# The second four images of an attention-weighted 3x3 convolution computed with four products per pair of output columns, on factor images made by GpSimd

## Chip, cores and metric

The kernel runs on one core of a Trainium2 chip. The metric is the device time of one execution in microseconds (us). A core has the engines TensorE (PE; its weight loads are listed as PEld), VectorE (DVE), ScalarE (ACT), GpSimd (POOL) and SyncE (SP), which here issues nearly all DMAs. All data are float32.

## What is computed

`x` has the shape (8, 32, 64, 64): 8 images, 32 channels, 64x64 pixels. Two stages follow each other, both with a residual. The first is a spectral convolution on the lowest 32x32 modes; the change doesn't touch it. The second is a 3x3 convolution whose kernel is mixed for every image from 16 kernels by an attention over the image's mean:

```
x = x + spectral_conv(group_norm(x))
v = group_norm(x)                                   # one group per channel
att = softmax(sigmoid(mean_hw(v) @ ksm_w.T))        # (8, 16)
kernels = clip(ifft2(sum_k att[b,k] * dft_weight[k]).real, -10, 10)
x = x + (conv3x3(v, kernels, padding=1) + bias) * fbm_scale
```

## The kernel before

**Layout.** After the spectral stage the result lies as `xa` (in `y_buf`): partition 32j + c holds channel c of the image rows 4u + j (u from 0 to 15), 66 columns per row with a padding column at each end. `xb` (in `w_buf`) is `xa` with the partition halves swapped and shifted by one row group, made by two DMAs per image; with both, a product reaches three image rows in four matrix products that run side by side, each on 32 rows of output partitions. The images are worked in two groups of four, g = 0 (images 0 to 3) and g = 1 (images 4 to 7): statistics, attention, aggregated kernel, weights, and then the convolution, one image after the other.

**The convolution** (`conv(b, n)`, line 1043) forms output columns in pairs with five products. Product n = 0 is shared by both columns: the middle kernel column on `sa` = pixel 1 + pixel 2 of each pair (made by GpSimd, in `x_buf`; its swapped copy lies in `t_buf` or `r_buf`). n = 1 is two more terms for the even columns, n = 2 two more for the odd ones, read from `xa` and `xb` at every second column. A term is eight matrix instructions of 512 columns (four row blocks, two passes for float32). The results go in turn into six PSUM banks (`conv_bank`). ScalarE takes product 0 with the bias into `shared` (`out_copy`, line 556); VectorE adds it to products 1 and 2 and writes the output rows in `bd_buf` (`out_copy`, line 816, two per image).

**What sets the order.** Each engine has its own list of work, written by hand, and the lists meet in semaphores. On TensorE: the inverse transforms i1 and i2 of the first stage, the small products of group 0's attention, its aggregation (line 1001), then `conv` of the images 0 to 7. Between the products of the images 0 to 3 stand group 1's small products: `sum_rows(1)` (line 982), `logits(1)` (line 987, waits for `pool_ready`, which VectorE's line 728 gives), `spread(1)` (line 993, waits for `num_ready`, given by line 752), `aggregate(1)` (line 1001), `mean_through_kernels(1)` (line 1009). TensorE waits at each of these in its order. On VectorE, the steps of a group's attention are `variance` (lines 716 to 719), `pooled` (724 to 728), `scales` (732 to 740), `sigmoid` (745, 746), `by_group` (752), `attention` (760), then `kernels` (770 to 780) and the weight copies (794). Most of them are tiny, and each waits for the one before. Between `variance(1)` and `pooled(1)` stands `out_copy(0)`.

GpSimd, after the work on the 16 kernels, forms `sa` in four instructions of two images each (line 441). SP issues in this order: loads; for the images 0, 2, 1, 3 the copies to `xb`; their `sa` copies; copies to `xb` and of `sa` for 4, 6 and then 5, 7; then all stores, four of 128 KB per image (line 307), each image once VectorE has counted `out_dve` up to it. The last image is stored in halves, two of its four stores per half from ScalarE's queue.

## Time and profile before

| | |
|---|---|
| median of 3 runs | 139.88 us (139.41 to 140.42) |
| the profiled execution | 140.62 us |
| span in its profile, first to last instruction | 138.8 us |
| granted TensorE clock, mean | 0.995 |
| TensorE busy | 122.7 us (88%) |
| VectorE busy | 88.0 us (63%) |
| ScalarE busy | 70.7 us (51%) |
| GpSimd busy | 52.6 us (38%) |
| convolution, first to last product | about 94.2 to 134.7 us |

All times within the run are us from the start of the span. Busy time of an engine counts its instructions' spans, without the time in which it waits for a semaphore. An instruction that has been issued and is held up by a resource shows as a longer instruction.

### The profile page before, as it was taken

Reading aid. Unit: us, or ns where it says so; the run is one execution under the profiler, and the core shown is the slowest. Engines: PE = TensorE matmul, PEld = TensorE weight load, DVE = VectorE, ACT = ScalarE, POOL = GpSimd, SP = SyncE. Lnnn points to the kernel's source line nnn. Section 1 sums busy time; section 2 is a strip of 40 time slices with the busy share of each in tenths; the row PEclk is TensorE's granted clock in tenths of the full one; section 3 lists DMA queues with packets and bytes.
Section 4 is the critical chain, followed back from the end, with each engine's and each line's share of the span. In section 5 each row is a group of like instructions: output and inputs, shape, how many; then the busy total and the mean of one; then the engine's idle time right before and its main releaser. Section 6 shows DMA issues by size and latency. Waiting matters only on the chain.

```text
span 138.8 us, 4752 instructions
## 1 busy us (share of the span) xinstructions
PE 122.7 (88%) x2028; PEld 93.4 (67%) x2028; DVE 88.0 (63%) x201; ACT 70.7 (51%) x142; POOL 52.6 (38%) x44
## 2 busy tenths in 40 slices
PE   0689997999998659979999979998999999999970
PEld 0679997899998549979999969883322423233440
DVE  0078687889969823633358675999882889922440
ACT  0487557548977014523317866654998429411100
POOL 7992000009969999999600460040500000000000
PEclk9999999999999999999999999999999999999998
DMA  3999988999900067688682899988989988773577
GB/s 87 261 226 236 248 191 280 310 378 401 340 9 7 5 152 174 144 189 190 153 191 47 169 175 171 202 202 171 201 173 173 200 185 180 171 156 86 115 157 146
DMA packets 71892, 25.17 MB, mean 181 GB/s; under 512 B 67904, under 2 KB 68160, under 8 KB 71872
## 3 DMA queue, kind: packets, MB, share of 16 engines
q1 hardware_dynamic: 70784, 24.62, 76.6%
q10 hardware_dynamic: 1088, 0.26, 0.9%
q8 instruction: 16, 0.26, 0.8%
q14 instruction: 4, 0.03, 0.1%
HBM read 14.38 MB, written 4.19 MB: 134 GB/s over the span
## 4 chain that ended last, share of the span: by engine, by line
PE 80%; issue 6%; DVE 5%; DMA 3%; ACT 2%; SPq 1%; DVEq 0%; ACTq 0%
PE slot L1043 27%; PE slot L956 10%; PE slot L877 10%; PE slot L971 8%; PE slot L899 5%; PE slot L936 5%; PE slot L945 5%; PE aggp L1001 3%; DMA x_buf<-x 3%; PE slot L903 2%; PE aggp L899 1%; PE small L899 1%; ACT L459 1%; DVE row_sq L611 1%; ACT q_buf L459 1%
## 5 line engine op out<-in xcount | busy, mean ns | idle before, releaser
L1043 PE MATMUL slot<-w_buf,conv_w 128*32 128x512 f32 (+1 forms) x136 | 31.8, 602 | 0.0
L1043 PE MATMUL slot<-y_buf,conv_w 128*32 128x512 f32 (+1 forms) x136 | 31.7, 602 | 0.0
L877 PE MATMUL slot<-cst,x_buf 128*64 128x64 f32 x512 | 18.2, 234 | 5.9 <-DMA x_buf<-x 4.6
L877 PEld LDWEIGHTS slot<-cst,x_buf 128*64 128x64 f32 x512 | 17.5, 148 | 6.3 <-issue 6.2
L816 DVE TENSOR_TENSOR bd_buf<-slot,q_buf 128x512 f32<-128x512 f32 (+1 forms) x17 | 11.1, 672 | 9.3 <-PE slot L1043 8.9
L441 POOL TENSOR_TENSOR x_buf<-y_buf 128x1024 f32<-128x1024 f32 x4 | 7.7, 1940 | 23.1 <-DVE y_buf L704 23.1
L971 PE MATMUL slot<-cst,t_buf 128*128 128x128 f32 x128 | 15.5, 278 | 0.8 <-issue 0.8
L971 PEld LDWEIGHTS slot<-cst,t_buf 128*128 128x128 f32 x128 | 14.7, 192 | 1.4 <-issue 1.2
L1043 PEld LDWEIGHTS slot<-y_buf,conv_w 128*32 128x32 f32 x136 | 8.8, 109 | 9.9 <-issue 9.6
L956 PE MATMUL slot<-cst,r_buf 128*64 128x128 f32 x256 | 14.6, 274 | 0.7 <-ACT r_buf L489 0.7
L611 DVE TENSOR_REDUCE row_sq<-q_buf 128x16 f32<-128x1024 f32 (+1 forms) x9 | 9.8, 1098 | 8.4 <-ACT q_buf L459 8.1
L956 PEld LDWEIGHTS slot<-cst,r_buf 128*64 128x64 f32 x256 | 13.9, 137 | 1.1 <-ACT r_buf L489 0.9
L1043 PEld LDWEIGHTS slot<-w_buf,conv_w 128*32 128x32 f32 x136 | 9.4, 109 | 7.7 <-issue 7.3
L504 ACT ACTIVATE q_buf<-y_buf 128x512 f32<-128x512 f32 x16 | 10.0, 624 | 7.5 <-DVE y_buf L704 7.5
L704 DVE SCALAR_TENSOR_TENSOR y_buf<-slot,stat,x_buf 128x512 f32<-128x512 f32 x16 | 11.2, 747 | 2.4 <-PE slot L971 2.4
L547 ACT ACTIVATE conv_w<-kern 32x160 f32<-32x160 f32 x24 | 8.0, 334 | 6.7 <-DVE kern L780 6.2
L378 POOL MEMSET x_buf<- 128x4096 f32 x1 | 3.5, 3516 | 19.6 <-DVE bd_buf L661 19.6
L556 ACT ACTIVATE q_buf<-slot,st 128x512 f32<-128x512 f32 x8 | 5.5, 682 | 10.1 <-PE slot L1043 6.1
L694 DVE COPY t_buf<-slot 128x512 f32<-128x512 f32 x8 | 5.5, 691 | 7.4 <-PE slot L956 7.4
L459 ACT ACTIVATE q_buf<-x_buf 128x1024 f32<-128x1024 f32 (+1 forms) x9 | 8.6, 959 | 1.5 <-DMA x_buf<-x 1.4
L495 ACT ACTIVATE t_buf<-slot 128x512 f32<-128x512 f32 x8 | 4.8, 594 | 8.2 <-PE slot L956 8.2
L1043 PE MATMUL slot<-x_buf,conv_w 128*32 128x512 f32 x32 | 8.4, 596 | 0.0
(125 smaller groups left out, 222.5 us busy)
## 6 DMA issues: line engine op xcount, KB each, us to landing
x_buf<-x SPq DMA_DIRECT2D x16, 256.0 KB, 4.4
w_buf<-w_modes SPq DMA_DIRECT2D x16, 256.0 KB, 5.4
x_buf<-x SPq DMA_DIRECT2D x32, 128.0 KB, 3.1
w_buf<-y_buf SPq DMA_DIRECT2D x16, 256.0 KB, 5.5
out<-bd_buf SPq DMA_DIRECT2D x28, 128.0 KB, 2.8
t_buf<-dft_w SPq DMA_DIRECT2D x4, 288.0 KB, 6.5
t_buf<-x_buf SPq DMA_DIRECT2D x8, 128.0 KB, 3.1
r_buf<-x_buf SPq DMA_DIRECT2D x8, 128.0 KB, 3.7
```

The source lines that it names most:

```text
L441: nc.gpsimd.tensor_tensor(sa[:, bs], xa[:, bs, :, 1:W + 1:2], xa[:, bs, :, 2:W + 2:2], ALU.add).then_inc(s_ready, 1)
L459: act.activation(sq, src, ACT.Square).then_inc(sq_ready, 1)
L504: act.activation(sq_trash[:, 512 * y:512 * y + 512].rearrange("p (u w) -> p u w", u=8), xa[:, 4 * g + 2 * y + x, 8 * half:8 * half + 8, 1: ...
L547: act.activation(cw[1][32 * j:32 * j + 32, 4 * g + i], kt[32 * i:32 * i + 32, :, kh], ACT.Copy).then_inc(w1_ready, 1)
L611: nc.vector.tensor_reduce(dst, sq, AX_X, ALU.add).then_inc(sq_used, 1)
L704: nc.vector.scalar_tensor_tensor(out=xa[:, b, us, 1:W + 1], in0=ps[:, :, y, :], scalar=mean1[:, b:b + 1], in1=xr[:, b, us, :], op0=ALU.sub ...
L816: nc.vector.tensor_tensor(rows[:, us, :, y], own[:, us], common[:, us], ALU.add).then_inc(out_dve, 1)
L877: last = pe.matmul(ps[64 * ri:64 * ri + 64, col:col + 64], x_part(k)[:, i, q, :], const("fwd_h")[:, 64 * ri:64 * ri + 64], start=True, sto ...
L899: last = pe.matmul(ps[:, col:col + 64], y_rows[:, b, f:f + 4, :].rearrange("w g c -> w (g c)"), const("fwd_w")[:, 0:64], start=True, stop= ...
L956: last = pe.matmul(ps[64 * ri:64 * ri + 64, 128 * i:128 * i + 128], r_modes[:, g, c0 + i].rearrange("p y n -> p (y n)"), const(matrix), st ...
L971: last = pe.matmul(ps[:, 128 * u:128 * u + 128], t_rows[:, g, x, h:h + 4, :].rearrange("p j c -> p (j c)"), const("inv_w"), start=True, st ...
L1043: last = pe.matmul(ps[32 * j:32 * j + 32, 32 * u0:32 * u1], cw[r][:, b, k, :], src, start=(k == terms[0][0]), stop=(k == terms[-1][0]))
```

## The change

Images 4 to 7 are convolved with four products per pair of output columns, each a single term. With d0 to d3 the four input columns of a pair and k0, k1, k2 the kernel's columns:

```
P0 = (k0 + k1 + k2) * (d1 + d2)     P1 = (k0 - k1 + k2) * (d2 - d1)
P2 = k0 * (d0 - d2)                 P3 = k2 * (d1 - d3)
even column = P0/2 + P1/2 + P2      odd column = P0/2 - P1/2 - P3
```

The parts:

- GpSimd makes four factor images (`plain`, 0: d0-d2, 1: d1-d3, 2: d1+d2, 3: d2-d1) for each pair of images, eight instructions of the size of line 441 where there were two, and sets the edge rows of their copies to zero. The last four wait for the side padding of group 1 (`pads_ready` 7), which ScalarE writes from the statistics of group 1.
- SP copies the factor images with their halves swapped in 16 DMAs of 256 KB instead of 8 of 256 KB and 8 of 128 KB. Source and target runs are 2 KB instead of 256 bytes for `xb`. They stand in front of the stores.
- VectorE makes the summed kernels of group 1 in three chained steps instead of one, and takes an image's products with four instructions instead of two (one more for the last image in both).
- ScalarE splits `pads(1)` into `side_pads(1)` (one instruction, put in front of the weights of images 2 and 3) and `row_pads(1)` (two instead of five).
- TensorE runs 15 full products and two halves for images 4 to 7, each of one term, instead of 4 products of one term and 8 of two.

```diff
@@ -337,20 +359,26 @@
                 for j in range(4):
                     sp.dma_start(xr[32 * j:32 * j + 32, b],
                                  x[b].rearrange("c (u j) w -> j c u w", j=4)[j]).then_inc(xr_in[2 * (b // 4) + b % 2], 16)
-            for n, b in enumerate((0, 2, 1, 3, 4, 6, 5, 7)):
+            for n, b in enumerate((0, 2, 1, 3)):
 
                 sp.wait_ge(xa_ready, 4 * (n // 2 + 1))
                 sp.dma_start(xb[0:64, b, 1:UB + 1, 1:W + 1], xa[64:128, b, :, 1:W + 1]).then_inc(xb_in[b], 16)
                 sp.dma_start(xb[64:128, b, 0:UB, 1:W + 1], xa[0:64, b, :, 1:W + 1]).then_inc(xb_in[b], 16)
-                if n in (3, 5, 7):
-                    for i in ((0, 2, 1, 3) if n == 3 else (4, 6) if n == 5 else (5, 7)):
-                        sp.wait_ge(s_ready, 2 * (i // 4) + i % 2 + 1)
-                        sp.dma_start(sb_of[i // 4][0:64, i % 4, 1:UB + 1], sa[64:128, i]).then_inc(sb_in[i], 16)
-                        sp.dma_start(sb_of[i // 4][64:128, i % 4, 0:UB], sa[0:64, i]).then_inc(sb_in[i], 16)
+            for b in (0, 2, 1, 3):
+                sp.wait_ge(s_ready, b % 2 + 1)
+                sp.dma_start(sb0[0:64, b, 1:UB + 1], sa[64:128, b]).then_inc(sb_in[b], 16)
+                sp.dma_start(sb0[64:128, b, 0:UB], sa[0:64, b]).then_inc(sb_in[b], 16)
+            sp.wait_ge(e_zero, 3)
+            for n, (k, a) in enumerate(((0, 2), (1, 2), (0, 0), (1, 0))):
+                sp.wait_ge(e_ready, 2 * n + 2)
+                for i in (k, k + 2):
+                    to, landed = (sums4[:, i], sb_in[4 + i]) if a else (diffs(i), xb_in[4 + i])
+                    sp.dma_start(to[0:64, :, 1:UB + 1], plain[k][64:128, i // 2, a:a + 2]).then_inc(landed, 16)
+                    sp.dma_start(to[64:128, :, 0:UB], plain[k][0:64, i // 2, a:a + 2]).then_inc(landed, 16)
             for b in range(B):
                 parts = 2 if b == B - 1 else 1
                 for n in range(parts):
-                    sp.wait_ge(out_dve, 2 * b + 2 + n)
+                    sp.wait_ge(out_dve, 2 * b + 2 if b < 4 else 4 * b - 4 + n)
                     for j in range(4 // parts):
                         store(sp, b, j, slice(UB // parts * n, UB // parts * (n + 1)))
             for k in range(3):
...
@@ -434,12 +462,28 @@
 
             nc.gpsimd.memset(tap_n[:, :, 288:289], 3.0).then_inc(taps_ready, 1)
 
-            for g in range(2):
-                for k in range(2):
-                    gp.wait_ge(xa_ready, 8 * g + (4 * k + 4 if g else 8))
-                    bs = slice(4 * g + k, 4 * g + k + 3, 2)
-                    nc.gpsimd.tensor_tensor(sa[:, bs], xa[:, bs, :, 1:W + 1:2], xa[:, bs, :, 2:W + 2:2],
-                                            ALU.add).then_inc(s_ready, 1)
+            for k in range(2):
+                gp.wait_ge(xa_ready, 8)
+                bs = slice(k, k + 3, 2)
+                nc.gpsimd.tensor_tensor(sa[:, bs], xa[:, bs, :, 1:W + 1:2], xa[:, bs, :, 2:W + 2:2],
+                                        ALU.add).then_inc(s_ready, 1)
+
+            def pixels(k, c):
+
+                return xa[:, 4 + k:7 + k:2, :, c:c + W - 1:2]
+
+            for k in range(2):
+                gp.wait_ge(xa_ready, 12 + 4 * k)
+                nc.gpsimd.tensor_tensor(plain[k][:, :, 2], pixels(k, 1), pixels(k, 2), ALU.add).then_inc(e_ready, 1)
+                nc.gpsimd.tensor_tensor(plain[k][:, :, 3], pixels(k, 2), pixels(k, 1), ALU.subtract).then_inc(e_ready, 1)
+                if k == 0:
+                    gp.wait_ge(i2_done, 8)
+                    for edge in (sums4[:, :, 1, 0:UB + 1:UB], diffs_r[:, :, :, 0:UB + 1:UB], diffs_t[:, :, 0:UB + 1:UB]):
+                        nc.gpsimd.memset(edge, 0.0).then_inc(e_zero, 1)
+            gp.wait_ge(pads_ready, 7)
+            for k in range(2):
+                nc.gpsimd.tensor_tensor(plain[k][:, :, 0], pixels(k, 0), pixels(k, 2), ALU.subtract).then_inc(e_ready, 1)
+                nc.gpsimd.tensor_tensor(plain[k][:, :, 1], pixels(k, 1), pixels(k, 3), ALU.subtract).then_inc(e_ready, 1)
 
         @block.scalar
         def _(act):
...
@@ -573,10 +626,11 @@
             squares(7, 7)
             out_copy(0)
             finish_stats(1)
+            side_pads(1)
             weights(0, 2, 3)
             softmax(1)
             out_copy(1)
-            pads(1)
+            row_pads(1)
             out_copy(2)
             weights(1, 0, 1)
             out_copy(3)
...
@@ -777,8 +831,13 @@
                     scalar=-CLIP, in1=scale_in[:].unsqueeze(1).broadcast_to([128, 9, 32]), op0=ALU.max, op1=ALU.mult))
 
                 chain(nc.vector.tensor_tensor(sets[:, 1, 1], sets[:, 1, 1], eye32, ALU.add))
-                nc.vector.tensor_tensor(sets[:, 3:5], sets[:, 0:3:2], sets[:, 1:2].broadcast_to([128, 2, 3, 32]),
-                                        ALU.subtract).then_inc(kern_ready, 1)
+                if g == 0:
+                    nc.vector.tensor_tensor(sets[:, 3:5], sets[:, 0:3:2], sets[:, 1:2].broadcast_to([128, 2, 3, 32]),
+                                            ALU.subtract).then_inc(kern_ready, 1)
+                else:
+                    chain(nc.vector.tensor_tensor(sets[:, 3], sets[:, 0], sets[:, 2], ALU.add))
+                    chain(nc.vector.tensor_tensor(sets[:, 4], sets[:, 3], sets[:, 1], ALU.subtract))
+                    nc.vector.tensor_tensor(sets[:, 3], sets[:, 3], sets[:, 1], ALU.add).then_inc(kern_ready, 1)
                 v.wait_ge(kern_ready, g + 1)
 
             def kernel_sums(g):
...
@@ -807,13 +866,28 @@
                     v.wait_ge(stored[b % 4], 64)
                 elif b == 2:
                     v.wait_ge(taps_ready, 1)
-                for y in range(2):
+                if b < 4:
+                    for y in range(2):
+                        own = conv_bank(b, 1 + y).rearrange("p (u q) -> p u q", u=UB)
+                        v.wait_ge(conv_done, product(b, 1 + y) + 1)
+                        nc.vector.tensor_tensor(rows[:, :, :, y], own, common, ALU.add).then_inc(out_dve, 1)
+                    return
+                taken = 4 * b - 8
+                for y, sign in ((0, 0.5), (1, -0.5)):
+                    own = conv_bank(b, 1).rearrange("p (u q) -> p u q", u=UB)
+                    v.wait_ge(conv_done, product(b, 1) + 1)
+                    nc.vector.scalar_tensor_tensor(out=rows[:, :, :, y], in0=own, scalar=sign, in1=common,
+                                                   op0=ALU.mult, op1=ALU.add).then_inc(out_dve, 1)
+                for y, sign in ((0, 1.0), (1, -1.0)):
                     parts = 2 if (b, y) == (B - 1, 1) else 1
                     for n in range(parts):
                         us = slice(UB // parts * n, UB // parts * (n + 1))
-                        own = conv_bank(b, 1 + y + n).rearrange("p (u q) -> p u q", u=UB)
-                        v.wait_ge(conv_done, 3 * b + 2 + y + n)
-                        nc.vector.tensor_tensor(rows[:, us, :, y], own[:, us], common[:, us], ALU.add).then_inc(out_dve, 1)
+                        own = conv_bank(b, 2 + y + n).rearrange("p (u q) -> p u q", u=UB)
+                        v.wait_ge(conv_done, product(b, 2 + y + n) + 1)
+                        v.wait_ge(out_dve, taken + 1 + y)
+                        nc.vector.scalar_tensor_tensor(out=rows[:, us, :, y], in0=own[:, us], scalar=sign,
+                                                       in1=rows[:, us, :, y], op0=ALU.mult,
+                                                       op1=ALU.add).then_inc(out_dve, 1)
 
             for k in range(5):
                 copy_t(k)
...
@@ -1014,30 +1088,39 @@
 
                 g, i = divmod(b, 4)
                 u0, u1 = rows.start, rows.stop
+                p = product(b, n + (u0 > 0))
                 if n == 0:
                     if i == 0:
                         pe.wait_ge(w_zero, 2)
-                        pe.wait_ge(pads_ready, 6 * (g + 1))
+                        pe.wait_ge(pads_ready, 6 if g == 0 else 9)
+                        if g:
+                            pe.wait_ge(e_zero, 3)
                     pe.wait_ge(w0_ready, 3 * (b + 1))
                     pe.wait_ge(w1_ready, 3 * (b + 1))
-                    pe.wait_ge(s_ready, 2 * g + i % 2 + 1)
+                    if g == 0:
+                        pe.wait_ge(s_ready, i % 2 + 1)
                     pe.wait_ge(sb_in[b], 32)
-                if n == 1:
+                if n == g + 1:
+                    if g:
+                        pe.wait_ge(e_ready, 6 + 2 * (i % 2))
                     pe.wait_ge(xb_in[b], 32)
-                if b < 2:
-                    pe.wait_ge(xa_ready, 2 * (6 + (3 * b + n) // 2))
-                elif n == 0:
-                    pe.wait_ge(out_act, b - 1)
+                if p < 6:
+                    pe.wait_ge(xa_ready, 2 * (6 + p // 2))
                 else:
-                    pe.wait_ge(out_dve, 2 * (b - 2) + n)
-                if u0:
-                    pe.wait_ge(out_act, b)
+                    taken, value = conv_taken(p - 6)
+                    pe.wait_ge(taken, value)
                 ps = conv_bank(b, n + (u0 > 0))
-                terms = (((1, None),), ((0, 0), (4, 2)), ((3, 1), (2, 3)))[n]
+                if g == 0:
+                    terms = (((1, None),), ((0, 0), (4, 2)), ((3, 1), (2, 3)))[n]
+                else:
+                    terms = ((3, 2), (4, 3), (0, 0), (2, 1))[n:n + 1]
                 for k, col in terms:
                     for j, (r, shifted, u) in enumerate(((1, True, 0), (0, False, 0), (1, False, 0), (0, True, 1))):
-                        if col is None:
-                            src = sb_of[g][:, i, u + u0:u + u1] if shifted else sa[:, b, u0:u1]
+                        if g:
+                            moved = sums4[:, i, col - 2] if col >= 2 else diffs(i)[:, col]
+                            src = moved[:, u + u0:u + u1] if shifted else plain[i % 2][:, i // 2, col, u0:u1]
+                        elif col is None:
+                            src = sb0[:, i, u + u0:u + u1] if shifted else sa[:, b, u0:u1]
                         else:
                             src = (xb if shifted else xa)[:, b, u + u0:u + u1, col:col + W - 1:2]
                         last = pe.matmul(ps[32 * j:32 * j + 32, 32 * u0:32 * u1], cw[r][:, b, k, :], src,
```

GpSimd's list from its last step on the 16 kernels, before, with the semaphores that each instruction waits for (`x_buf` holds `sa`, `y_buf` holds `xa`):

```order
L399 TENSOR_SCALAR bd_buf<-bd_buf 128x384 [waits pool_done] x2
L396 TENSOR_TENSOR bd_buf<-bd_buf 128x384 [waits pool_done]
L396 TENSOR_TENSOR taps<-bd_buf 128x3x4x32 [waits pool_done] x2
L435 MEMSET taps 128x4 [waits pool_done]
L441 TENSOR_TENSOR x_buf<-y_buf 128x2x512 [waits xa_ready] x4
```

The same place of the changed kernel (`w_buf` and `x_buf` now hold `plain[0]` and `plain[1]`):

```order
L468 TENSOR_TENSOR x_buf<-y_buf 128x2x512 [waits xa_ready] x2
L477 TENSOR_TENSOR w_buf<-y_buf 128x2x512 [waits xa_ready]
L478 TENSOR_TENSOR w_buf<-y_buf 128x2x512
L482 MEMSET t_buf 128x4x2x32 [waits i2_done]
L482 MEMSET r_buf 128x6x2x32
L482 MEMSET t_buf 128x2x2x32
L477 TENSOR_TENSOR x_buf<-y_buf 128x2x512 [waits xa_ready]
L478 TENSOR_TENSOR x_buf<-y_buf 128x2x512
L485 TENSOR_TENSOR w_buf<-y_buf 128x2x512 [waits pads_ready]
L486 TENSOR_TENSOR w_buf<-y_buf 128x2x512
L485 TENSOR_TENSOR x_buf<-y_buf 128x2x512
L486 TENSOR_TENSOR x_buf<-y_buf 128x2x512
```

Of the four `sa` instructions the two of group 1 are gone, and eight stand in their place: one directly behind the first at each of the two places, and four at the end behind a wait of their own.

SP's list around the first store, before:

```order
L343 DMA w_buf<-y_buf 64x16x64 [waits xa_ready]
L344 DMA w_buf<-y_buf 64x16x64
L348 DMA r_buf<-x_buf 64x512 [waits s_ready]
L349 DMA r_buf<-x_buf 64x512
L348 DMA r_buf<-x_buf 64x512 [waits s_ready]
L349 DMA r_buf<-x_buf 64x512
L307 DMA out<-bd_buf 512x1x64 [waits out_dve]
```

And of the changed kernel:

```order
L376 DMA r_buf<-w_buf 64x2x512 [waits e_ready]
L377 DMA r_buf<-w_buf 64x2x512
L376 DMA r_buf<-w_buf 64x2x512
L377 DMA r_buf<-w_buf 64x2x512
L376 DMA r_buf<-x_buf 64x2x512 [waits e_ready]
L377 DMA r_buf<-x_buf 64x2x512
L376 DMA t_buf<-x_buf 64x2x512
L377 DMA t_buf<-x_buf 64x2x512
L329 DMA out<-bd_buf 512x1x64 [waits out_dve]
```

The first store stands behind the copies of the last factor images, which wait for GpSimd's last instruction (`e_ready` 8).

VectorE's list at the change from the weights to image 4, before:

```order
L816 TENSOR_TENSOR bd_buf<-slot,q_buf 128x512 [waits conv_done]
L799 TENSOR_TENSOR st<-st,small 128x4 [waits bias_done]
L794 COPY conv_w<-kern 32x160 x6
L816 TENSOR_TENSOR bd_buf<-slot,q_buf 128x512 [waits conv_done,stored0,out_act]
L816 TENSOR_TENSOR bd_buf<-slot,q_buf 128x512 [waits conv_done]
```

And of the changed kernel:

```order
L873 TENSOR_TENSOR bd_buf<-slot,q_buf 128x512 [waits conv_done]
L858 TENSOR_TENSOR st<-st,small 128x4 [waits bias_done]
L853 COPY conv_w<-kern 32x160 x6
L879 SCALAR_TENSOR_TENSOR bd_buf<-slot,q_buf 128x512 [waits conv_done,stored0,out_act]
L879 SCALAR_TENSOR_TENSOR bd_buf<-slot,q_buf 128x512 [waits conv_done]
L888 SCALAR_TENSOR_TENSOR bd_buf<-slot,bd_buf 128x512 [waits out_dve,conv_done] x2
```

The place is the same; per image there are four instructions over 512 elements instead of two.

## Rows read from the trace of the kernel before

**Rows 1.** The page, part 1: busy us (share of the span) xinstructions.

```profile
PE 122.7 (88%) x2028; PEld 93.4 (67%) x2028; DVE 88.0 (63%) x201; ACT 70.7 (51%) x142; POOL 52.6 (38%) x44
```

**Rows 2.** The chain that ended last, in time: start us, us, engine, tile, line.

```profile
91.28 0.94 DVE kern L775
...
92.47 0.37 DVE kern L780
...
94.22 2.90 PE slot L1043 x20
...
116.15 18.51 PE slot L1043 x173
...
134.68 0.43 DVE bd_buf L816
```

**Rows 3.** Timeline of TensorE, images 5 to 7: start us, us, engine, line, operation.

```profile
120.56 0.59 PE L1043 MATMUL slot<-x_buf,conv_w 128*32 128x512 f32 x1
...
121.42 0.63 PE L1043 MATMUL slot<-y_buf,conv_w 128*32 128x512 f32 x1
...
129.78 0.59 PE L1043 MATMUL slot<-x_buf,conv_w 128*32 128x512 f32 x1
```

**Rows 4.** Timeline of GpSimd, 47 us, and 70 us to the end.

```profile
47.46 1.20 POOL L399 TENSOR_SCALAR bd_buf<-bd_buf 128x384 f32<-128x384 f32 x1
...
78.27 3.83 POOL L441 TENSOR_TENSOR x_buf<-y_buf 128x1024 f32<-128x1024 f32 x2 [9.86 <-DVE y_buf L704]
89.97 1.92 POOL L441 TENSOR_TENSOR x_buf<-y_buf 128x1024 f32<-128x1024 f32 x1 [7.86 <-DVE y_buf L704]
97.29 1.95 POOL L441 TENSOR_TENSOR x_buf<-y_buf 128x1024 f32<-128x1024 f32 x1 [5.40 <-DVE y_buf L704]
```

**Rows 5.** Timeline of VectorE: instructions beside GpSimd's, and their twins of group 1.

```profile
48.17 0.29 DVE L677 TENSOR_TENSOR fc_diag<-prm,cst 128x128 f32<-128x128 f32 x1
...
81.15 0.97 DVE L718 TENSOR_TENSOR st<-st 128x4 f32<-128x4 f32 x1
...
100.79 0.16 DVE L718 TENSOR_TENSOR st<-st 128x4 f32<-128x4 f32 x1
...
112.67 0.46 DVE L775 SCALAR_TENSOR_TENSOR kern<-kern,scale_in 128x288 f32<-128x288 f32 x1
```

**Rows 6.** Timeline of VectorE, `pooled(1)` to `by_group(1)`.

```profile
102.27 0.15 DVE L724 SCALAR_TENSOR_TENSOR st<-st 128x4 f32<-128x4 f32 x1
...
102.67 0.16 DVE L728 TENSOR_TENSOR st<-st 128x4 f32<-128x4 f32 x1
...
103.20 0.22 DVE L737 SCALAR_TENSOR_TENSOR st<-stat,bconst,st 128x4 f32<-128x4 f32 x1
...
106.13 0.17 DVE L752 TENSOR_TENSOR soft<-soft,cst 16x16 f32<-16x16 f32 x1 [0.27 <-ACT soft L518]
```

**Rows 7.** Timeline of TensorE, `logits(1)` and `spread(1)`.

```profile
103.97 0.17 PE L987 MATMUL small<-st,prm 128*16 128x4 f32 x1
...
106.84 0.39 PE L993 MATMUL small<-soft,cst 16*128 16x16 f32 x2
```

**Rows 8.** Timeline of ScalarE: standard deviation of group 1, side padding of `xa`.

```profile
101.57 0.21 ACT L510 ACTIVATE st<-st 128x4 f32<-128x4 f32 x1
...
106.57 0.36 ACT L538 ACTIVATE y_buf<-st 128x128 f32<-128x128 f32 x1
```

**Rows 9.** Timeline of SP's DMA issues.

```profile
90.03 0.60 SPq L349 DMA_DIRECT2D t_buf<-x_buf  x1
...
109.16 4.80 SPq L307 DMA_DIRECT2D out<-bd_buf  x7
...
109.16 26.92 SPq L307 DMA_DIRECT2D out<-bd_buf  x32
```

**Rows 10.** The page, part 5: VectorE's residual addition, of the shape of the new output instructions.

```profile
L704 DVE SCALAR_TENSOR_TENSOR y_buf<-slot,stat,x_buf 128x512 f32<-128x512 f32 x16 | 11.2, 747 | 2.4 <-PE slot L971 2.4
```

**Rows 11.** Timeline of VectorE: the last weight copies, in front of image 4's output.

```profile
118.05 2.02 DVE L794 COPY conv_w<-kern 32x160 f32<-32x160 f32 x6
```

63 lines of the change are left out of this document (43 added, 20 removed).

## The prediction

> **What bounds the kernel now.** I read the page's busy shares first, then the chain that ended last, then the timelines of each engine from 75 us on. TensorE is busy 88% of the span [rows 1], and in the convolution it is the bound outright: the chain of the images 4 to 7 is one run of TensorE work, 18.51 us from 116.15, and ends in a single VectorE output of 0.43 us [rows 2]. So fewer products there pay at once. In front of that run the chain passes through small VectorE instructions on which TensorE waits: `kernels(0)`, 91.28 to 92.84 [rows 2], stands directly ahead of the first product at 94.22. Group 1's small steps are not on the chain, but close: line 728 ends at 102.83 [rows 6] and TensorE comes to `logits(1)` at 103.97 [rows 7], 1.14 us of slack; line 752 ends at 106.30 [rows 6] and `spread(1)` starts at 106.84 [rows 7], 0.54 us. GpSimd has 38% of work [rows 1], and after 78 us just four instructions of about 1.92 us [rows 4].
>
> **What the removed products give.** A product of one term takes 121.42 - 120.56 = 0.86 us; an image of five terms takes (129.78 - 120.56)/2 = 4.61 us [rows 3], that is 0.94 per term of the two-term products. All new sources are contiguous, as those of the 0.86 us term are, so an image takes 4 x 0.86 = 3.44 us. The four images took 134.66 - 116.0 = 18.66 us [rows 2]; I take 13.85 (the last product in halves adds a tenth). **-4.8 us.** With 0.94 per term it would be -3.7; the first is nearer in layout.
>
> **What GpSimd's added work does to VectorE.** This decides the case. Eight instructions of 1.92 us replace two, plus three memsets. No product waits for their results: the last copies are issued by 114.6 (below), and the products that read them come after 121. But rows 5 show what else a GpSimd tensor_tensor does. Line 718, four elements, takes 0.16 us in group 1 and 0.97 in group 0, where it was issued at 81.15 beside GpSimd's pair that ends at 82.10 [rows 4, 5]; it ends at 82.12. Line 775 takes 0.46 us in group 1 [rows 5] and 0.94 in group 0 [rows 2], issued at 91.28 beside the GpSimd instruction that ends at 91.89 [rows 4]. Both have two inputs in SBUF; both end as if they had started 0.14 us before GpSimd's end. So a VectorE instruction with two SBUF inputs is held until a running GpSimd tensor_tensor is nearly done. The row that speaks against it is line 677, two SBUF inputs, 0.29 us at 48.17 beside a GpSimd tensor_scalar [rows 4, 5]: not held. All new GpSimd arithmetic is tensor_tensor. If only the two held rows count, the sum is the one below; if line 677 is taken as the rule, the stalls fall away, and it is 137.7 us (first rival). The Trainium skill ("SBUF — State Buffer", section "Who interferes with whom") states that such a VectorE instruction and a GpSimd instruction that reads SBUF exclude each other for a whole instruction, whichever starts first. By that rule the sum is the one below; the rule doesn't tell tensor_tensor from tensor_scalar, and there line 677 disagrees with it.
>
> Which of two queued instructions gets in when GpSimd has its next one ready, no row shows. I take turns: VectorE gets in at a GpSimd end, since a held instruction started 0.14 us before that end, and GpSimd then restarts. Now in time:
>
> 1. `kernels(0)`. GpSimd's second instruction now follows the one of 89.97 at once. Line 775 gets in as before and ends at 92.21; GpSimd holds from there to 94.1; lines 779 and 780 (0.37 us, [rows 2]) follow and end at 94.6 instead of 92.84. The first product moves by **+1.75**. VectorE and ScalarE are dense or fed by VectorE here, so everything behind moves with it.
> 2. `logits(1)`. Line 510 on ScalarE ends at 101.78 [rows 8], now 103.55; the side padding takes 0.36 [rows 8]; GpSimd's last four start at about 104.0 and run to 112. Line 724 would start at 102.27 + 1.75, and a little later, since line 718 is held once more: 104.3. It is held to 105.9. Line 728 behind it is held by the next GpSimd instruction to 107.85 and then gives `pool_ready`. TensorE stands at `logits(1)` from 103.97 + 1.75 = 105.7: **+2.15**. Behind it in TensorE's list stand all other products.
> 3. `spread(1)`. Lines 732 and 733 ride along with 728; line 737 is held to 110.0, line 752 to 112.0. TensorE, going on at 108.1 with three terms (2.8 us), comes at 110.9 and waits to 112.1: **+1.2**.
>
> Together **+5.1**. Hidden: `kernels(1)` has two more small chained steps (about 0.45 us, from 0.46 and 0.37 us for 288 and 192 elements [rows 5, 2]); the first product of image 4 has about 1 us of cover, `mean_through_kernels(1)` 0.4: **+0.1**. The earlier side padding (0.36 us) delays only weight copies with over 0.7 us in hand: nothing. If that cover were gone it would cost its 0.36.
>
> **What stands behind TensorE.** VectorE now takes four instructions per image. Their shape is line 704's, 11.2/16 = 0.70 us each [rows 10], so 2.8 us per image, under TensorE's 3.44. But VectorE comes to image 4 only at the end of its copies, 118.05 + 2.02 [rows 11], and with +5.2 at 125.3; image 4 is out at 128.1, then 130.9, 133.7, 136.6. SP stands in front of the stores with the last four copies, which wait for GpSimd's end: 112.0, and four issues of about 0.65 us (0.60 for the last copies, [rows 9]) make 114.6 for the first store instead of 109.16 [rows 9]. A store takes 4.80/7 = 0.69 us. Twelve end at 122.9, image 3's (ready 118 + 5.2) at 125.9, those of 4, 5 and 6 at 130.9, 133.7 and 136.5, the four half stores of image 7 at about 138.3. Before, the last issue ended at 109.16 + 26.92 = 136.08 [rows 9]. What lies behind the last issue stays. **Sum: 138.3 - 136.1 = +2.2 us**: -4.8 + 5.2 from TensorE, and +1.8 because VectorE and the stores have no gaps left to catch up in. The profiled execution goes from 140.62 to 142.8; it lies 0.74 above the median, so the median goes from 139.88 to **142.1 us**.
>
> **Rivals.**
>
> - **No holding up** (faster). Line 677 is the general case and the two long rows have another cause. Then GpSimd ends at 102.1 + 4 x 1.92 = 109.8, the first store goes out at 112.5, TensorE ends at about 130. Now the stores bind: 28 x 0.70 + 4 x 0.45 = 21.4 us end at 133.9, -2.2: 137.7 us. The 4.8 us can't be had in full, since the store queue starts late. It decides if line 728 ends before TensorE reaches `logits(1)`. Chance 0.22.
> - **Line 724 and 728 slip past** (same). Line 724 (104.3) and GpSimd's first of four (104.0) are 0.3 us apart. If 724 wins, 728 is held by one instruction less and `logits(1)` loses about 0.2 us, `spread(1)` about 0.8: the shift is 2.8 instead of 5.2, the stores bind from 114.3, the last issue ends at 135.8: 139.6 us. Chance 0.18.
> - **Taking turns within the small steps too**. If GpSimd also gets in between 728, 732 and 733 (issued 0.07 us apart), `spread(1)` waits 1.4 us more: 143.5 us. Chance 0.12.
> - **GpSimd keeps its turn** through its four. Line 724 is held to 111.6, `logits(1)` to 112.2: +6.4, with +1.95 from `kernels(0)`; `spread(1)` is covered. VectorE comes to image 4 at 128.5 and ends at 139.8: about 145.2 us. For it: the pair at 78.27 takes 3.83, with no gap [rows 4]. Against it: no VectorE instruction was waiting there. Chance 0.08.
>
> My forecast has 0.40.
>
> **Numbers.** A change of about 1% (1.4 us) is what a measurement of this kernel can tell from none. The forecast and its two worse variants give slower: 0.40 + 0.12 + 0.08 = 0.60, less 0.04 for a forecast whose sum is 1 us too high. The side-step and that rest give same: 0.22. No holding up lies at -1.6%: 0.22 faster. The range reaches from no holding up to turns within the small steps, 137.4 to 143.7, and leaves out the last rival and the tails. For the forecast alone: 141.0 to 143.2, by 0.94 us per term above and half a microsecond on each stall.
>
> **What the changed profile would show.** Right: lines 779/780 of group 0 end near 94.6 and one of them is about 1.9 us long; the second group's 724, 728, 737 and 752 are 1.5 to 1.9 us long beside GpSimd's last four; TensorE idles over 2 us at `logits(1)` and 1 at `spread(1)`; an image of group 1 takes 3.4 to 3.5 us; the first store is issued after 114. Wrong in the first step, if these VectorE rows keep their lengths of 0.15 to 0.22 us. Wrong in the second, if images take 3.7 us, or if TensorE waits for `out_dve` inside them. Wrong in the third, if the stores have gaps between images 4 and 7.

## The result, and the profile after

The changed kernel takes 145.41 us (median of 4 runs, 144.40 to 146.94) against 139.64 us for the kernel before on the same chip (139.10 to 140.42): ratio 1.036, 95% interval 1.031 to 1.041. Medians here and below are of all runs of a kernel, while ratios and intervals leave out runs more than 1.5% above that kernel's fastest, so a ratio can differ a little from the quotient of two medians. The profiled execution has a span of 143.0 us, against 138.8. It comes to `kernels(0)` 0.79 us earlier than the profiled execution before did (its first instruction starts at 89.22 instead of 90.01), which has nothing to do with the change; differences below that are called "aligned" allow for it.

The page after, part 1, answers to [rows 1]:

```profile
PE 121.1 (85%) x1988; PEld 92.6 (65%) x1988; DVE 100.6 (70%) x211; ACT 69.2 (48%) x139; POOL 64.9 (45%) x53
```

The timeline of GpSimd after, 85 us to the end, without three short memsets, answers to [rows 4]:

```profile
89.18 1.94 POOL L477 TENSOR_TENSOR w_buf<-y_buf 128x1024 f32<-128x1024 f32 x1 [7.87 <-DVE y_buf L758]
91.06 2.12 POOL L478 TENSOR_TENSOR w_buf<-y_buf 128x1024 f32<-128x1024 f32 x1
...
102.93 1.94 POOL L485 TENSOR_TENSOR w_buf<-y_buf 128x1024 f32<-128x1024 f32 x1 [1.04 <-ACT y_buf L574]
104.83 1.92 POOL L486 TENSOR_TENSOR w_buf<-y_buf 128x1024 f32<-128x1024 f32 x1
106.71 1.93 POOL L485 TENSOR_TENSOR x_buf<-y_buf 128x1024 f32<-128x1024 f32 x1
108.60 1.93 POOL L486 TENSOR_TENSOR x_buf<-y_buf 128x1024 f32<-128x1024 f32 x1
```

The timeline of VectorE after. Lines 829, 833, 835 are 775, 779, 780 of before; lines 778, 782, 786, 787, 791 and 806 are 724, 728, 732, 733, 737 and 752 [rows 2, 5, 6]:

```profile
90.48 0.94 DVE L829 SCALAR_TENSOR_TENSOR kern<-kern,scale_in 128x288 f32<-128x288 f32 x1
91.46 1.77 DVE L833 TENSOR_TENSOR kern<-kern,cst 128x32 f32<-128x32 f32 x1
93.26 0.36 DVE L835 TENSOR_TENSOR kern<-kern 128x192 f32<-128x192 f32 x1
...
103.23 1.67 DVE L778 SCALAR_TENSOR_TENSOR st<-st 128x4 f32<-128x4 f32 x1
...
105.14 1.63 DVE L782 TENSOR_TENSOR st<-st 128x4 f32<-128x4 f32 x1
106.69 0.15 DVE L786 TENSOR_TENSOR st<-st,cst 128x4 f32<-128x4 f32 x1
106.77 1.89 DVE L787 TENSOR_TENSOR st<-st,cst 128x4 f32<-128x4 f32 x1
...
108.88 1.66 DVE L791 SCALAR_TENSOR_TENSOR st<-stat,bconst,st 128x4 f32<-128x4 f32 x1
...
111.48 0.17 DVE L806 TENSOR_TENSOR soft<-soft,cst 16x16 f32<-16x16 f32 x1 [0.27 <-ACT soft L562]
```

Each of the four-element instructions of 1.6 to 1.9 us ends within 0.1 us of a GpSimd end (104.87, 106.75, 108.64, 110.53): the two engines take turns. Four elements that took 0.15 us take 1.67.

The timeline of TensorE after: `logits(1)` (line 1061) and `spread(1)` (line 1067), as in [rows 7]:

```profile
106.83 0.20 PE L1061 MATMUL small<-st,prm 128*16 128x4 f32 x2 [1.85 <-DVE st L782]
...
111.70 0.39 PE L1067 MATMUL small<-soft,cst 16*128 16x16 f32 x2 [0.17 <-DVE soft L806]
```

The chain that ended last, after, answers to [rows 2]. The small VectorE steps of group 1, which were not on it, now are, and images 4 to 7 are one run of 13.55 us instead of 18.51. (The chain leaves TensorE for VectorE before the last half product is done. That product ends at 135.22, so TensorE's work on the four images spans 13.95 us, against 18.49 before.)

```profile
105.14 1.63 DVE st L782
106.84 1.82 DVE st L787
108.88 1.67 DVE st L791
111.70 0.39 PE small L1067 x2
...
121.27 13.55 PE slot L1126 x128
```

The stores after, as in [rows 9], and what SP waited for from 100 us on (engine, line, releaser: us in all, times, longest), first after, then before:

```profile
113.55 27.54 SPq L329 DMA_DIRECT2D out<-bd_buf  x32
```

```profile
SPq L329 <- DVE bd_buf L888: 2.1, 1, 2.1
...
SPq L329 <- DVE bd_buf L873: 0.7, 2, 0.5
...
SPq L329 <- DVE bd_buf L879: 0.3, 1, 0.3
```

```profile
SPq L307 <- DVE bd_buf L816: 5.9, 5, 2.1
```

Two of the waits after (0.5 of L873, 0.3 of L879) are put down to outputs that come later than the one that the store needs, so 2.3 to 3.1 us were spent waiting. Without the waits the 32 stores took 24.4 to 25.2 us after, 0.76 to 0.79 each, and 26.92 - 5.9 = 21.0 before, 0.66 each. The pace of an unhindered issue did not change: before, the first twelve stores went out in 8.31 us without a wait, 0.69 each, and most of those after take as long. What raises the mean are single long issues, in the last stretch these three above all (first the row of before, then the three):

```profile
109.16 8.31 SPq L307 DMA_DIRECT2D out<-bd_buf  x12
```

```profile
132.64 1.32 SPq L329 DMA_DIRECT2D out<-bd_buf  x1
...
137.65 1.16 SPq L329 DMA_DIRECT2D out<-bd_buf  x1
...
138.86 1.22 SPq L329 DMA_DIRECT2D out<-bd_buf  x1
```

The last two are half stores, which took 0.36 to 0.47 us before. The DMA engines' busy share is 0.91 from 132 to 134 us and again from 138 to 140; it was 0.95 from 134 to 136 before, with no long issue, so the share alone does not tell which issue is long.

### The profile page after: what moved, and what is told of

It is laid out like the page before. It is cut to its first block, busy times and chain, and to the rows that moved or that the text cites. A ratio compares the mean times of both kernels' runs of the same rounds, so it can differ in the third digit from the quotient of the medians.

```text
span 143.0 us, 4697 instructions
## 1 busy us (share of the span) xinstructions
PE 121.1 (85%) x1988; PEld 92.6 (65%) x1988; DVE 100.6 (70%) x211; ACT 69.2 (48%) x139; POOL 64.9 (45%) x53
## 4 chain that ended last, share of the span: by engine, by line
PE 71%; DVE 16%; issue 5%; DMA 2%; ACT 1%; DVEq 0%; SPq 0%
PE slot L1126 14%; PE slot L951 13%; PE slot L1030 10%; PE slot L1045 8%; PE slot L1010 6%; PE slot L973 5%; PE slot L1019 5%; PE aggp L1075 3%; DVE conv_w L853 2%; DMA x_buf<-x 2%; DVE y_buf L758 2%; PE slot L977 2%; PE aggp L973 1%; DVE st L787 1%; PE small L973 1%
## 5 line engine op out<-in xcount | busy, mean ns | idle before, releaser
L1126 PE MATMUL slot<-w_buf,conv_w 128*32 128x512 f32 x96 | 24.7, 650 | 0.0
L951 PE MATMUL slot<-cst,x_buf 128*64 128x64 f32 x512 | 18.9, 237 | 4.4 <-DMA x_buf<-x 4.2
L951 PEld LDWEIGHTS slot<-cst,x_buf 128*64 128x64 f32 x512 | 18.1, 151 | 4.9 <-issue 4.7
L1126 PE MATMUL slot<-y_buf,conv_w 128*32 128x512 f32 x64 | 17.3, 678 | 0.0
L1126 PE MATMUL slot<-t_buf,conv_w 128*32 128x512 f32 (+1 forms) x60 | 13.9, 570 | 2.4 <-DVE conv_w L853 2.3
L1126 PE MATMUL slot<-x_buf,conv_w 128*32 128x512 f32 (+1 forms) x52 | 11.6, 568 | 0.0
L1126 PEld LDWEIGHTS slot<-w_buf,conv_w 128*32 128x32 f32 x96 | 6.2, 113 | 7.9 <-issue 7.9
L1126 PEld LDWEIGHTS slot<-t_buf,conv_w 128*32 128x32 f32 x60 | 4.1, 109 | 8.7 <-issue 7.3
L1019 PE MATMUL slot<-fc_diag,q_buf 128*128 128x128 f32 x64 | 7.4, 276 | 1.0 <-DVE q_buf L724 1.0
```

Of the source, the lines that this page charges most:

```text
L951: last = pe.matmul(ps[64 * ri:64 * ri + 64, col:col + 64], x_part(k)[:, i, q, :], const("fwd_h")[:, 64 * ri:64 * ri + 64], start=True, sto ...
L1019: last = pe.matmul(ps[:, 512 * half + 128 * bb:512 * half + 128 * bb + 128], mixed[:, 2 * k + half, 2 * bb:2 * bb + 2].rearrange("p b m g ...
L1126: last = pe.matmul(ps[32 * j:32 * j + 32, 32 * u0:32 * u1], cw[r][:, b, k, :], src, start=(k == terms[0][0]), stop=(k == terms[-1][0]))
```

## Where the time goes in every kernel

One table carries the comparisons: us from the first instruction of `kernels(0)` to image 4's first product, from there to the end of SP's last store issue, and from there to the end of the span, in the profiled execution of each kernel (labels as in the experiments below; runs 4 and 9 are not in it).

| kernel | to image 4 | image 4 to last store | rest | sum |
|---|---|---|---|---|
| before | 26.1 | 19.9 | 2.7 | 48.8 |
| after | 32.1 | 19.8 | 1.9 | 53.8 |
| 1 GpSimd's work added to before | 31.7 | 20.0 | 2.7 | 54.5 |
| 2 first pair later | 30.0 | 19.7 | 1.9 | 51.6 |
| 3 last four as memsets | 29.6 | 19.9 | 1.9 | 51.3 |
| 5 stores of images 0, 1 early | 33.0 | 19.6 | 1.8 | 54.4 |
| 6 late copies left out | 33.0 | 20.3 | 1.8 | 55.2 |
| 7 GpSimd timed | 26.3 | 24.4 | 2.2 | 52.8 |
| 8 timed, stores early | 26.4 | 22.3 | 2.2 | 50.9 |
| 10 four terms, stores early | 26.2 | 16.8 | 2.9 | 45.9 |
| 11 four terms, four outputs | 26.2 | 18.2 | 2.9 | 47.3 |
| 12 as 8, late copies left out | 26.4 | 20.3 | 2.2 | 48.9 |
| 13 as 7, late copies left out | 26.4 | 21.3 | 2.2 | 49.8 |

The change lost 5.9 us ahead of image 4 and won 0.1 us from there to the last store and 0.8 behind it, although TensorE's work there shrank by 4.5. Small differences from "before" are to be read with care: the profiled execution before took 140.62 us, while the medians before in the batches below lie between 139.56 and 140.48.

## Experiments

**1. GpSimd's work alone, in the old kernel.** Six tensor_tensor instructions of GpSimd, of the size and at the places of the change's, write to a free stretch of `t_buf`.

```diff
                     nc.gpsimd.tensor_tensor(sa[:, bs], ..., ALU.add).then_inc(s_ready, 1)
+                    if g == 1:
+                        nc.gpsimd.tensor_tensor(free, xa[...], xa[...], ALU.add).then_inc(extra, 1)
+            gp.wait_ge(std2_ready, 2)
+            for k in range(4):
+                nc.gpsimd.tensor_tensor(free, xa[...], xa[...], ALU.add).then_inc(extra, 1)
```

> The kernel before, with nothing changed but GpSimd: six more tensor_tensor instructions of 1.92 us, writing to a free part of t_buf that nobody reads, one behind each of group 1's two sa instructions and four behind group 1's standard deviation. Their times are those of the changed kernel's factor images; the convolution keeps five products. Theory (GpSimd's tensor_tensor holds VectorE's instructions with two SBUF inputs): line 779 about 1.8 us long, lines 724, 728, 733, 737 1.6 to 1.9 us each; first product 1.6 us later, logits(1) 3.6 us, spread(1) 5.6 us, and the whole +5.2 to +5.8 us, 145.1 us. Rival (the loss of the changed kernel comes from VectorE's two more outputs per image and the late stores, the long rows are incidental): within 1% of 139.6 us.

Measured: 146.85 against 139.56 us, ratio 1.053 (1.048 to 1.059). Image 4 comes 5.6 us later, and nothing but GpSimd's list was touched, so GpSimd's added instructions alone make a loss as large as the whole change's. The medians are 7.3 us apart, the profiled executions 6.1; what the rest beyond the 5.6 is made of was not looked into. VectorE's and GpSimd's timelines of this kernel (lines 735, 739, 744, 748 are 724, 728, 733, 737 of before):

```profile
104.26 1.37 DVE L735 SCALAR_TENSOR_TENSOR st<-st 128x4 f32<-128x4 f32 x1
...
105.88 1.75 DVE L739 TENSOR_TENSOR st<-st 128x4 f32<-128x4 f32 x1
...
107.62 0.15 DVE L744 TENSOR_TENSOR st<-st,cst 128x4 f32<-128x4 f32 x1
...
108.00 1.64 DVE L748 SCALAR_TENSOR_TENSOR st<-stat,bconst,st 128x4 f32<-128x4 f32 x1
109.67 1.99 DVE L751 TENSOR_SCALAR scale_in<-prm,st 128x32 f32<-128x32 f32 x1
```

```profile
103.66 7.97 POOL L451 TENSOR_TENSOR t_buf<-y_buf 128x1024 f32<-128x1024 f32 x4 [0.74 <-ACT st L521]
```

Here 733 did ride along with 728, as I had predicted for the change, where it was held 1.89 us. The traces show a difference in order. In this run each added GpSimd instruction waits for the one before it, which leaves 0.08 us between them, and line 744 starts at 107.62, 0.06 us before GpSimd's next. In the changed kernel and in runs 2, 5 and 6 the same line starts 0.06 us after GpSimd's next and takes 1.89 to 1.90 us. That the earlier of the two wins fits all five; but 0.02 us ahead was not enough for line 751 below, and no run was made to vary it. Line 751, a tensor_scalar with one tensor input, was held too, to 111.66, GpSimd's end at 111.63.

**2. The first pair of factor instructions after `kernels(0)`.**

```diff
             for k in range(2):
                 gp.wait_ge(xa_ready, 12 + 4 * k)
+                if k == 0:
+                    gp.wait_ge(kern_ready, 1)
```

> The changed kernel with one more wait: GpSimd's first two factor instructions start only when kernels(0) is done. Theory of the hold: lines 829, 833, 835 take 0.46, 0.19 and 0.36 us, the first product comes 1.6 us earlier, and since the later stretch keeps its pattern, the end comes 1.6 us earlier: 143.6 us, ratio to before 1.025. Rival (the start of the convolution isn't what the end hangs on, but the stores are): the stores start when GpSimd is done, which also moves by 1.6 us, so only where GpSimd's end doesn't move with it do the two differ; if less than 0.8 us comes back, the shift is absorbed behind it.

Measured: 143.21 us, ratio 1.031 (1.021 to 1.040); the three steps take 0.46, 0.19 and 0.36 us again, and image 4 comes 2.1 us earlier than in the changed kernel; the profiled execution is 2.2 us shorter (1.6 were expected). The two ratios lie closer (1.036 and 1.031), with intervals that overlap, so the profile carries this verdict.

**3. The last four factor instructions as memsets** (constants in place of the differences of pixels).

```diff
-                nc.gpsimd.tensor_tensor(plain[k][:, :, 0], pixels(k, 0), pixels(k, 2), ALU.subtract)...
+                nc.gpsimd.memset(plain[k][:, :, 0], 1.0)...
```

> The kernel of e2 again (the last four factor images are made by memsets that read nothing; their values are wrong), since in e2's single execution TensorE ran at half clock from 30 to 42 us. From kernels(0) to the end e2 took 52.0 us against 53.8 in the changed kernel and 48.8 in the one before. So about 1.8 us less than the changed kernel: 142.9 us, ratio 1.023. If the hold at logits(1) and spread(1) were all that the change costs: 4 us less, 140.6 us.

Measured: 143.60 against 140.21 us, ratio 1.023 (1.015 to 1.030). Of the two-input steps none is held, but line 794, a tensor_scalar, is: it ends with the memset beside it. VectorE, then GpSimd:

```profile
105.02 0.15 DVE L787 TENSOR_TENSOR st<-st,cst 128x4 f32<-128x4 f32 x1
...
105.66 1.03 DVE L794 TENSOR_SCALAR scale_in<-prm,st 128x32 f32<-128x32 f32 x1
```

```profile
105.70 0.96 POOL L485 MEMSET x_buf<- 128x1024 f32 x1
```

Of the 4.1 us that the holds at `logits(1)` and `spread(1)` had cost, image 4 gets back 2.5. One reason stands in the windows of this run: behind the 2.3 us of idleness at `kernels(0)` TensorE's granted clock was 0.73, 0.50 and 0.91 in the stretches from 94 to 100 us, where the changed kernel had 1.00.

In an earlier single run of this kernel TensorE had half its clock from about 33 to 46 us, in code that the change doesn't touch; its small steps had the same lengths (0.15 to 0.22 us), and its time (151.13 us) says nothing.

**4. The same four with one input** (a copy of pixels by a tensor_scalar instead of a difference).

```diff
+                nc.gpsimd.tensor_scalar(plain[k][:, :, 0], pixels(k, 0), 1.0, None, ALU.mult)...
```

> The changed kernel with the last four factor instructions replaced by tensor_scalar instructions of the same size (one input, times 1.0); the output is wrong by these factors. It asks what line 677 left open. If only GpSimd's two-input instructions hold VectorE (line 677 is the rule): lines of pooled(1) and scales(1) 0.15 to 0.22 us as with the memset. If every GpSimd instruction that reads SBUF holds it: each as long as GpSimd's instruction, by line 399's 1.17 us for 384 elements about 3 us, so logits(1) later than in the changed kernel, and about 148 us.

A single run, 147.55 us, which is near the 148 expected if VectorE were held, but comes about in another way: GpSimd's form takes 2.87 us each, and the copies and stores that wait for it start late (first store at 117.81). What matters are VectorE's rows beside the instructions that run from 103.46 to 114.86:

```profile
103.97 0.64 DVE L778 SCALAR_TENSOR_TENSOR st<-st 128x4 f32<-128x4 f32 x1
...
104.85 0.16 DVE L782 TENSOR_TENSOR st<-st 128x4 f32<-128x4 f32 x1
...
105.01 0.16 DVE L787 TENSOR_TENSOR st<-st,cst 128x4 f32<-128x4 f32 x1
```

```profile
103.46 2.87 POOL L485 TENSOR_SCALAR w_buf<-y_buf 128x1024 f32<-128x1024 f32 x1 [2.03 <-ACT y_buf L574]
```

Line 782 starts and ends inside GpSimd's instruction. So line 677 in [rows 5] was no accident: in these traces two-input steps are held by GpSimd's two-input form, and by its one-input form for half a microsecond at most. The Trainium skill ("SBUF — State Buffer", section "Who interferes with whom") says that a VectorE instruction with two SBUF inputs contends with a GpSimd instruction that reads SBUF. The traces agree where GpSimd has two inputs (1.63 to 1.89 us) and where it only writes (0.15), and not where it reads one (0.16).

**5. Stores of images 0 and 1 ahead of the last two groups of copies.** My theory for what I had missed was that the stores start too late (113.55).

```diff
             for n, (k, a) in enumerate(((0, 2), (1, 2), (0, 0), (1, 0))):
+                if n >= 2:
+                    sp.wait_ge(out_dve, 2 * n - 2)
+                    for j in range(4):
+                        store(sp, n - 2, j, slice(0, UB))
```

> The changed kernel with SP's list reordered: the stores of image 0 stand in front of the third group of factor copies, those of image 1 in front of the fourth, nothing else. GpSimd's holding of VectorE stays as it is. Theory (two causes: the hold delays the products, and the stores, late behind the copies, use up what the four products give back): TensorE ends where it did in the changed kernel (13.5 us after image 4 starts), but two images' stores, about 5.5 us of issue, are out of the last stretch; the last issue comes some 3 us earlier, 142.0 us, ratio to before about 1.018. Rival (the hold alone sets the end): no more than 0.5 us comes back.

Measured: 146.19 against 139.90 us, ratio 1.043 (1.037 to 1.050). A miss: nothing comes back. From image 4's first product to the last store it is 19.6 us, against 19.8 in the changed kernel. There SP had waited 2.1 us for image 4's output with all earlier stores issued, so its late start had already been made up.

**6. The last eight copies left out** (differences of pixels across the halves are wrong then).

```diff
-            for n, (k, a) in enumerate(((0, 2), (1, 2), (0, 0), (1, 0))):
+            for n, (k, a) in enumerate(((0, 2), (1, 2))):
```

> The changed kernel without the last eight factor copies (the swapped halves of d0-d2 and d1-d3); TensorE reads what lies there, so the output is wrong by these halves. The stores stand behind only the first eight copies. Theory of two causes: stores start when image 0 is out (about 104 instead of 113.6), and the end follows VectorE's last output by about 2.5 us as in the kernel before: about 141.0 us. It bounds what any reordering of SP can bring while the hold stays. Rival (hold alone): as the changed kernel, 144.5.

Measured: 146.78 us, ratio 1.040 (1.027 to 1.052). A miss again, and 20.3 us behind image 4. SP stands 11.0 us at outputs of images 0 to 3 that aren't there yet: with image 4 late by 6 us, the first four images' stores and all copies fit in front of it. The theory of the late store start falls for this kernel. In both runs image 4 came 1 us later still. TensorE's clock did that: after the 2.3 us of idleness at `kernels(0)` it was granted half. A row of the windows of run 5 (busy us and counts by engine, then granted clock, DMA share, GB/s):

```profile
96.00:98.00 2.00, 2.00 (x16) 0.56 (x12) 2.00 (x7) 0.97 (x3) 0.00 (x0) 0.50 0.96 237
```

**7. All of GpSimd's instructions at places where no awaited two-input step runs.** The first pair after `kernels(0)`; the differences of images 4 and 6 early, but for the columns that need the padding; the rest after the small steps. Nothing is left out.

```diff
+            gp.wait_ge(xa_ready, 12)
+            gp.wait_ge(kern_ready, 1)
+            factor(0, 2, 1, 2, ALU.add)
+            factor(0, 3, 2, 1, ALU.subtract)
 ...
+            factor(0, 0, 0, 2, ALU.subtract, slice(1, 32), e_part)
+            factor(0, 1, 1, 3, ALU.subtract, slice(0, 31), e_part)
+            gp.wait_ge(pads_ready, 7)
+            gp.wait_ge(dve, 34)
 ...
+            factor(1, 2, 1, 2, ALU.add)
+            gp.wait_ge(num_ready, 2)
+            factor(1, 3, 2, 1, ALU.subtract)
+            factor(1, 0, 0, 2, ALU.subtract)
+            factor(1, 1, 1, 3, ALU.subtract)
```

> The changed kernel with the same eight factor images, but GpSimd's instructions put where VectorE has no short instruction with two SBUF inputs that somebody waits for: images 4 and 6 behind kernels(0), with the padded columns done later by two small instructions; then a wait to the end of scales(1), one instruction, a wait to by_group(1), three instructions. Copies of d0-d2, d1-d3 of images 4 and 6 stand before those of 5 and 7. Stores stay behind all copies. Theory of two causes: lines 829 to 835, 778, 782, 787, 791, 806 take 0.15 to 0.46 us; image 4 starts 0.5 us later than in the kernel before (its product count saves 4.9 us, TensorE ends 4.4 us earlier), but the first store is issued at about 113 and the stores end within 1 us of the kernel before's: 139.0 to 140.5 us. Rival (hold alone): 4.4 us faster than before, 135.2 us.

Measured: 144.77 us, ratio 1.034 (1.026 to 1.042), a miss for both the theory (139.0 to 140.5) and its rival (135.2). The front is mended (26.3 us to image 4, as before the change), and the time is hardly better: the loss has moved behind image 4, 24.4 us. The stores start at 116.39, behind the last copies, and image 4's output waits. The profile names no releaser for that; the instruction stands behind the wait for `stored[0]`, and image 0's stores landed at about 123.6, so I take it for the buffer that they read. SP's stores, and VectorE's wait:

```profile
116.39 25.25 SPq L329 DMA_DIRECT2D out<-bd_buf  x32
```

```profile
123.62 1.29 DVE L893 SCALAR_TENSOR_TENSOR bd_buf<-slot,q_buf 128x512 f32<-128x512 f32 x2 [1.99 <-issue]
```

**8. The same, with the stores of images 0 and 1 between the copies.**

```diff
+                if n in (0, 2):
+                    sp.wait_ge(out_dve, n + 2)
+                    for j in range(4):
+                        store(sp, n // 2, j, slice(0, UB))
```

> The previous kernel, with the stores of image 0 in front of the second group of copies and those of image 1 in front of the last. Theory of two causes: 2.5 to 3 us less than the previous one, 137.0 us, ratio to before 0.981, since now VectorE's outputs (about 2.8 us per image) and the stores bind together. Rival (hold alone): the same as the previous one within 0.5 us.

Measured: 142.29 us, ratio 1.019 (1.010 to 1.029): the best complete version with four products, and still slower than before. It is 2.5 us below run 7, as expected, but far from the expected 137.0. TensorE ends 4.2 us earlier than before the change (aligned), but the last store 2.6 us later. The DMA engines are full (busy share 0.98 to 1.03), and the last image's output waits for a buffer. Windows, then VectorE:

```profile
104.00:112.00 8.00, 7.65 (x58) 2.88 (x54) 5.96 (x14) 1.97 (x5) 6.13 (x4) 1.00 0.98 226
112.00:120.00 8.00, 7.90 (x80) 2.37 (x72) 7.37 (x21) 6.07 (x15) 0.00 (x0) 1.00 1.03 234
```

```profile
128.56 1.29 DVE L897 SCALAR_TENSOR_TENSOR bd_buf<-slot,q_buf 128x512 f32<-128x512 f32 x2 [1.56 <-DMA out<-bd_buf]
```

**9, 10, 11. Four terms in the old kernel.** The last term of images 4 to 7 is left out, with nothing else of the change; then also with image 0's stores ahead of image 7's copies; then (from 9) with each output of these images computed twice on VectorE.

```diff
-                terms = (((1, None),), ((0, 0), (4, 2)), ((3, 1), (2, 3)))[n]
+                terms = (((1, None),), ((0, 0), (4, 2)), ((3, 1), (2, 3)) if g == 0 else ((3, 1),))[n]
```

> The kernel before, with one thing taken away: the last term of the odd columns (kernel column 2) of the images 4 to 7. These images have four terms, as in the changed kernel; GpSimd, SP, ScalarE and VectorE do what they did. The output of these images lacks that term. It asks what four terms alone are worth. Theory A (TensorE's time counts in full up to the last image): 4 x 0.93 = 3.7 us less on TensorE, ratio to before about 0.974, 136.2 us. Theory B (behind TensorE stand four images of stores, 12.4 us from the moment image 4 is out, in every run in which TensorE is ahead): image 4 is out about 1 us earlier, then 12.4 us of stores instead of 14.55: 3.1 us at most, less what image 4's place in VectorE's list takes; 137.0 to 138.0 us.

> The previous kernel with image 0's stores put in front of the copies of image 7 in SP's list. If the stores' start at 109.2 matters once TensorE is faster (theory B with the queue's backlog), about 1 us less than the previous one. If only the last four images' own stores bind, the same within 0.5 us.

> e9's kernel (four terms, the last left out) with each of VectorE's outputs of the images 4 to 7 done twice, so four instructions per image as in the changed kernel, about 0.65 us each. GpSimd and SP unchanged. It prices the second added cost. VectorE comes to image 4 at 120 and needs 2.7 us per image: image 4 is out 1.3 us later, the others at its pace, and the stores follow with 2.7 us per image: 1.0 to 1.5 us more than e9. If TensorE or the stores cover the added outputs: the same as e9 within 0.5 us.

Measured against 140.21 us: 137.85 (0.974; 0.962 to 0.986), 137.76 (0.982; 0.975 to 0.990) and 139.17 us (0.989; 0.981 to 0.997). So the products are worth 1.8 to 2.6% (the 2.6 rests on two executions 1.9 us apart, the 1.8 on four), and image 0's earlier stores bring nothing. By the ratios the two more outputs take back 0.7 to 1.4%, with intervals that overlap; in the table it is 1.4 us behind image 4 (18.2 instead of 16.8), as expected. Even with no cost at all, the 3.8 us by which TensorE is shorter in run 10 (its last product ends at 130.05, 14.67 us after image 4's start, instead of 18.49) give 2.5 us by that run's ratio, since more of the stores now comes after its end. The chain of run 10, which leaves TensorE for VectorE at 129.10, before that product's end:

```profile
115.38 13.72 PE slot L1047 x118
129.23 1.02 DVE bd_buf L820 x2
```

**12, 13. Runs 8 and 7 with the last eight copies left out.**

```diff
-                for i in (k, k + 2):
+                for i in (k, k + 2) if a else ():
```

> The timed version with early stores (GpSimd's steps where VectorE has no two-input step waiting, stores of images 0 and 1 between the copies) again, but the last eight of the sixteen copies of factor images (those of the differences of columns, 256 KB each, 2 MB in all) are left out, and the convolution doesn't wait for them, so images 4 to 7 are computed with wrong differences across the halves. It stood at a ratio of 1.019, with last store issue to the end of the run as before. Theory A (the copies fill the DMA queue, on which the stores of all eight images wait): at 180 to 230 GB/s, which the trace shows there, 2 MB are 9 to 11 us of the queue, of which the old kernel had 1 MB (its shifted copies of sums and pixels for images 4 to 7 were 3 MB in all, the new ones are 4 MB); without them the run is 3 to 5 us shorter, ratio 0.985 to 0.995. Theory B (VectorE's four outputs per image and the waits for an output buffer to be stored set it, copies are hidden): nothing comes back, 1.015 to 1.02.

> The timed version with the stores in their old place behind all copies (ratio 1.034), with the same last eight copies left out and not waited for. Theory A (SP stands at the copies until 116, so that the stores begin late and VectorE waits for the first of the four output buffers): the stores begin some 5 us earlier, image 4's output no longer waits, and the run is 3 to 5 us shorter, ratio 0.99 to 1.01, about where the version with early stores and without those copies ends. Theory B (the queue of outputs on VectorE sets it): 1.03.

Measured against 140.48 us: 140.52 (1.0015; 0.997 to 1.006) and 140.10 us (1.0009; 0.997 to 1.005). The last eight copies cost 1.8% where the stores are early and 3.3% where they are late; without them it doesn't matter where the stores stand. Theory A holds. In run 12 its size was missed: 1.8% are 2.5 us, where 3 to 5 were expected. The eight copies are 2 MB, twice the 1 MB by which the change's copies exceed those of before, so these two runs move less than the old kernel does. In run 13 no output waits for a buffer. The first store still waits 0.7 us for GpSimd's last instruction, since that wait stayed in SP's list, and the 32 stores go out from 111.62 on with a single wait of 0.6 us:

```profile
111.62 25.12 SPq L329 DMA_DIRECT2D out<-bd_buf  x32
```

That is 0.77 us a store without the wait, and the kernel comes out where it was before the change. No complete version that beats the old kernel came out of these runs. One with four products for only two of the four images was not tried.

## Why the prediction was wrong

The direction, the mechanism of the hold and most of the front half were right; the size of what stands behind TensorE was not. By its own steps, aligned:

- *The removed products*, -4.8: 13.95 instead of 18.49 us, -4.5. Right to 0.3 us; half of that is the start of image 4, which I put at 116.0 where [rows 2] have 116.15.
- *`kernels(0)`*, +1.75: lines 833 and 835 end at 93.62 instead of 92.84, 0.78 + 0.79 = +1.57. Right, and run 2 gives it back (2.1 us).
- *`logits(1)`*, +2.15: 106.83 instead of 103.97, 2.86 + 0.79 - 1.57 = +2.08. Right. Each of 778 and 782 is held by one GpSimd instruction.
- *`spread(1)`*, +1.2: 111.70 instead of 106.84, 4.86 + 0.79 - 3.65 = +2.0. Line 787 did not ride along with 782 but was held for a turn of its own, which is one of the two extra holds of the rival "turns within the small steps". It was issued 0.06 us after GpSimd's next instruction had started (106.77 and 106.71); in run 1 the same line was issued 0.06 us ahead of that start, and rode along.
- *To image 4*, +0.1: 5.91 - 5.65 = +0.3.
- *Behind TensorE*, +1.8. Here is the failed step. TensorE ended 1.4 us later than before (135.22 instead of 134.64), the last store issue 5.8 later, so that the step costs 4.4, and 3.6 when 0.8 us less behind the last issue is taken off. The term that was mis-sized is the time of the stores. From image 4's output on I had stores of 0.69 us and half stores of 0.45: 10.2 us to the last. They took 12.5, from 128.60 to 141.09. (That output itself came at 128.58, aligned 1.3 us behind my 128.1, so the front and VectorE's way to it have a share in the miss too.) The 2.3 us are four issues: 132.64 with 1.32 us, 136.73 with 0.87, and two half stores with 1.16 and 1.22; the others took what I had put.

The 0.69 us were not misread; they are the pace at which SP issues, and not that at which stores land. Before, the first twelve stores were issued 0.69 us apart and landed 0.80 apart (111.84 to 120.65). The time from issue to landing grew from 2.7 to 3.8 us, and was back at 2.6 for image 4's first store, behind gaps in which SP waited for outputs (1.1 us up to there, 5.9 in all). Behind image 4 the changed kernel has no such gap: one full store or two halves, ScalarE's half stores included, landed every 0.75 us (131.18 to 142.48). My 0.45 for a half store also left out that ScalarE's queue stores as much again at the same time. That SP's issues grow long once stores land later than they are issued is my reading; no run separates it from other causes.

So the sum is +1.57 + 2.08 + 2.00 + 0.26 - 4.54 + 3.62 = +5.0 instead of +2.2: 1.8 of the 2.8 us missing are this step's, 0.7 the front's, most of it at `spread(1)`, and 0.3 the products'. The fourth rival, 145.2 us, names nearly the measured time by luck, with a mechanism that didn't happen: GpSimd did not keep its turn.

The rival "no holding up" failed twice. The hold is real (run 1), and where it was removed by placing GpSimd's work elsewhere (runs 7 and 8) the kernel was still 3.4 and 1.9% slower, not 1.6% faster. That rival had 21.4 us for all stores, where run 13, with a wait of 0.6 us, takes 25.1, and no cost for 1.05 MB of additional copies in front of them.

What the experiments show together: three costs lie side by side. The hold keeps image 4 back by 5.9 us; the copies and stores fill the DMA engines; VectorE's four outputs take 0.7 to 1.4%, which the intervals don't set clear of nothing. In the changed kernel the first hides the second (runs 5 and 6 win nothing), and with the first gone the second is the bound (runs 7 and 8 against 13 and 12). With the hold and eight copies gone the change is worth nothing: 1.001. What the remaining 1.2% between runs 12 or 13 and run 11 consist of was not taken apart; the largest difference in the traces is that the stores of images 4 to 7 take 13.0 us in run 12 (123.39 to 136.40) and 11.5 in run 11 (122.96 to 134.41). Run 12 has the long issues there again (1.87 us at 127.42), and run 11 none above 0.74.

## What to carry to other kernels

Work moved to an engine with idle time is free only if that engine runs beside nothing that others wait for: look for the awaited small VectorE steps with two inputs in the time window, and count one GpSimd instruction for each. Price a queue of stores by the pace at which they land where no gap lets them catch up, not by the pace at which they are issued: here 0.80 against 0.69 us. Count the stores of every queue that runs at the same time. When a bound engine gets less work, ask for each of the others behind it how much later than that engine it can start and how fast it can go; here the stores, which had waited 5.9 us for outputs, became the limit once outputs came faster.

## What was new about the hardware

- VectorE and GpSimd take turns: with GpSimd's instructions back to back, a held VectorE step of four elements took 1.63 to 1.89 us in the changed kernel, one GpSimd instruction, and never two. A step that started 0.06 us behind GpSimd's next instruction was held for that one too (changed kernel, runs 2, 5, 6); one that started 0.06 us ahead of it was not (run 1).
- GpSimd's one-input tensor_scalar held no two-input step for longer than 0.5 us (run 4), but takes 2.87 us where the two-input form takes 1.92; VectorE's tensor_scalar on 128x32 was held by GpSimd's two-input form (1.99 us, run 1), by its memset (1.03, run 3) and by its one-input form (0.71, run 4), against 0.24 us when GpSimd was idle.
- TensorE's granted clock was at the lower of its two levels (0.50, 1.2 GHz) soon after idle stretches of 1.9 to 2.3 us. In the changed kernel that was from 108 to 110 us, hidden by the wait at `spread(1)`; in runs 3 to 6 it was behind `kernels(0)` (2.26 or 2.27 us idle), and in runs 5 and 6 image 4 came 1 us later for it; the changed kernel and run 1 had the same stall there, 2.30 us, and kept 1.00. What decides it no run shows. A row of the windows after:

```profile
108.00:110.00 2.00, 2.00 (x16) 0.79 (x12) 1.93 (x3) 0.00 (x0) 2.00 (x2) 0.50 0.93 218
```
